# A gated cross-attention block on one core: one list of steps for all engines in place of a table of slots

## The reference

```python
def _L0_xattn_ref(query, context, ...):
    q = layer_norm(query, gq, betq)
    c = layer_norm(context, gkv, betkv)
    Q = (q @ Wq + bq) ; K = (c @ Wk + bk) ; V = (c @ Wv + bv)      # 16 heads
    attn = softmax(einsum('bhqd,bhkd->bhqk', Q, K) * SCALE)
    return einsum('bhqk,bhkd->bhqd', attn, V) @ Wo + bo
def _L0_ffn_ref(x, W1, b1, W2, b2):
    h = relu(x @ quantize(W1).T + b1)       # quantize: to -1, 0, 1 by a threshold on mean |W|
    return h @ quantize(W2).T + b2          # W1 2048 x 512, W2 512 x 2048
x = x + tanh(g_xattn[0]) * _L0_xattn_ref(_layernorm(x), ctx, ...)
x = x + tanh(g_ffn[0]) * _L0_ffn_ref(_layernorm(x), W1, b1, W2, b2)
```

## Time and profile before

| | |
|---|---|
| three runs | 1016.99, 1017.47, 1018.20 us; median 1017.47 us |
| the profiled execution | 1018.24 us, of which the span of instructions is 1016.4 us |
| PE busy | 917.1 us of the span, 90% |
| DVE, ACT, POOL busy | 735.9, 643.5, 307.8 us |
| mean granted clock of PE | 0.966 of full |

### The profile page before, as it was taken

How to read it: one execution, slowest core, us unless ns; L and a number is a source line. 1 busy time by engine, 2 the same in 40 slices (tenths; PEclk the granted TensorE clock), 3 DMA queues, 4 the chain that set the end, 5 groups by cost and what they waited for, 6 DMA issues and landing times.

```text
span 1016.4 us, 22463 instructions
## 1 busy us (share of the span) xinstructions
PE 917.1 (90%) x8994; PEld 704.0 (69%) x8994; DVE 735.9 (72%) x1358; ACT 643.5 (63%) x1330; POOL 307.8 (30%) x534
## 2 busy tenths in 40 slices
PE   3788898689999999999999999999999999889868
PEld 0444665466778778876788678876887677758747
DVE  4454699888777778777877877777877777788521
ACT  2765556755786567765795578756786576578411
POOL 4030265443250325122341325032412323033023
PEclk9798699889999999999999999999999999999969
DMA  9495925552211701251222411180223022210100
GB/s 292 129 247 132 217 75 143 144 147 39 50 38 46 172 21 41 62 150 33 60 63 66 117 41 39 45 182 7 55 62 101 2 60 62 65 38 1 37 4 19
DMA packets 56960, 84.02 MB, mean 83 GB/s; under 512 B 6376, under 2 KB 33448, under 8 KB 56856
## 3 DMA queue, kind: packets, MB, share of 16 engines
q1 hardware_dynamic: 50200, 65.80, 26.8%
q10 hardware_dynamic: 6656, 16.78, 5.6%
HBM read 42.20 MB, written 3.67 MB: 45 GB/s over the span
## 4 chain that ended last, share of the span: by engine, by line
PE 62%; DVE 8%; ACT 5%; POOL 2%; issue 1%; DMA 1%; SPq 1%; ACTq 0%
PE ps_fill L431 42%; PE ps_score L443 6%; PE ps_pv L472 5%; PE ps_exp L456 5%; DVE row_max L779 2%; PE ps_fill L482 2%; DVE p_parts L786 2%; ACT h_full L690 2%; PE ps_fill L524 1%; ACT ps_exp L642 1%; ACT ctx_raw L700 1%; POOL h_parts L1079 1%; DVE h_parts L882 1%; DMA x_residual<-x 1%; DVE rows_to_turn L804 1%
## 5 line engine op out<-in xcount | busy, mean ns | idle before, releaser
L640 ACT ACTIVATE p_parts<-ps_exp 125x448 f16<-125x448 f32 x384 | 209.0, 544 | 112.9 <-PE ps_exp L456 110.9
L779 DVE TENSOR_REDUCE row_max<-ps_score 128x1 f32<-128x750 f32 x256 | 237.9, 929 | 12.4 <-PE ps_score L443 10.1
L786 DVE TENSOR_TENSOR p_parts<-ps_exp,p_parts 125x448 f16<-125x448 f32 x384 | 235.5, 615 | 2.5 <-ACT ps_exp L642 2.5
L642 ACT ACTIVATE ps_exp<-ps_exp 125x448 f32<-125x448 f32 x384 | 210.8, 549 | 0.0
L443 PE MATMUL ps_score<-k_stack,q_stack 96*128 96x375 f16 x512 | 128.2, 332 | 43.1 <-DVE row_max L779 27.3
L456 PE MATMUL ps_exp<-q_stack,k_stack 99*125 99x224 f16 x768 | 141.3, 267 | 2.7 <-DVE p_parts L786 2.3
L456 PEld LDWEIGHTS ps_exp<-q_stack,k_stack 99*125 99x125 f16 x768 | 98.1, 140 | 35.4 <-DVE p_parts L786 9.0
L472 PE MATMUL ps_pv<-v_now,p_parts 125*128 125x66 f16 x3072 | 115.8, 194 | 1.1 <-DVE p_parts L786 1.1
L431 PE MATMUL ps_fill<-w_ternary,h_parts 128*128 128x256 fp8e4 x1024 | 116.5, 272 | 0.0
L472 PEld LDWEIGHTS ps_pv<-v_now,p_parts 125*128 125x128 f16 x3072 | 111.8, 98 | 1.2 <-issue 1.1
L431 PEld LDWEIGHTS ps_fill<-w_ternary,h_parts 128*128 128x128 f16 x1024 | 99.6, 98 | 11.2
(11 more groups left out here) (129 smaller groups left out, 1501.5 us busy)
## 6 DMA issues: line engine op xcount, KB each, us to landing
k_stack<-k_stage_hi SPq DMA_DIRECT2D x64, 187.5 KB, 2.7
v_now<-v_stage SPq DMA_DIRECT2D x32, 346.5 KB
ctx_raw<-ctx_in SPq DMA_DIRECT2D x8, 1344.0 KB
h_parts<-w1t ACTq DMA_DIRECT2D x16, 512.0 KB, 3.9
h_parts<-w2t ACTq DMA_DIRECT2D x16, 512.0 KB, 5.1
k_stack<-k_stage_lo SPq DMA_DIRECT2D x32, 187.5 KB, 3.2
x_for_q<-x SPq DMA_DIRECT2D x16, 256.0 KB, 11.1
x_residual<-x SPq DMA_DIRECT2D x16, 256.0 KB, 3.2
```

The costliest lines, as they stand in the source:

```text
L640: nc.scalar.activation(ph[0:KR, unit, :], ps_exp[0:KR, u, 0:2 * NQ], ACT.Exp, scale=EXP_SCALE)
L642: nc.scalar.activation(ps_exp[0:KR, u, 0:2 * NQ], ps_exp[0:KR, u, 0:2 * NQ], ACT.Exp, scale=EXP_SCALE).then_inc(exp_done, 1)
L779: nc.vector.tensor_reduce(mx[:, h, t:t + 1], ps_score[:, :, 0:KH], AX.XY, ALU.max) \
L786: nc.vector.tensor_tensor(pl[0:KR, unit, :], ps_exp[0:KR, u, 0:2 * NQ], ph[0:KR, unit, :], ALU.subtract).then_inc(p_split, 1)
```

## The change

The table of slots is gone. One list, `STEPS`, holds every step of the program as `kind.index@batch`: an opening of 791 steps, a round of 327 steps that is repeated for five batches, an ending of 330. Each engine walks the whole list and does its own part of what it finds. What was one step with a half on PE and ACT and a half on DVE is now two (`k` and `k_hi`, `cx` and `cx_lo`, `op` and `op_add`, `f2` and `f2_add`), the maximum is a step (`max`) apart from its `score`, the difference (`part`) apart from its `expo`, the sum of a `pv` is `take`, POOL's splitting of maxima is `split`; and every DMA is a step of SP: `kq`, `vc`, `ctx`, `x`, `xb`, `store`, `load`, `reload`.

Besides the order:

- PE no longer waits at the start of a body; each fill waits for the fill two ahead of it, and for nothing else of this kind.
- The 32 loads of weight pieces are issued by SP, not ACT. For the second pass they go through two buffers in place of three.
- The gates and the columns of small vectors are loaded by ACT's queue, ahead of everything; the rows `bo` and `b2` come after the weights.
- The first `rstd` and the last `rstd2` are done by DVE but for the power, which stays on POOL.
- `bo_sum` and `threshold` use `ps_fill`, the thresholds of W1 and W2 are made one by one, and the bias of q and k is turned by a DMA of its own.

The number of matmuls, of exponentials, of maxima and of comparisons is the same. The core of the diff:

```diff
-SLOT_WORK = [
-    [("q", 0), ("q", 1), ("mr", 1), ("bias", 0), ("divide", 0), ("k", 0)],
...
+ROUND = """
+    pv.12@-1 score.4@0 f2.2@-2 max.1@0 f2_add.0@-2 kq.1@0 part.36@-1 part.37@-1 take.11@-1 max.2@0 expo.42@-1 cx.4@1
...
+STEPS = steps_of(OPENING, 0)
+for _b in range(FIRST_ROUND, LAST_ROUND + 1):
+    STEPS += steps_of(ROUND, _b)
+STEPS += steps_of(ENDING, 0)
+FILLS = [s for s in STEPS if s[0] in FILL_KINDS]
+FILL_AT = {s: k for k, s in enumerate(FILLS)}
...
+                elif kind in FILL_KINDS:
+                    at = FILL_AT[kind, i, n]
+                    if at >= 2:
+                        pe.wait_ge(*freed(*FILLS[at - 2]))
+                    fill(kind, i, n, at % 2)
...
             def sum_piece(k):
 
-                act.wait_ge(piece_loaded[k % PIECE_RING], 16 * (k // PIECE_RING + 1))
-                nc.scalar.activation(piece[:, k % PIECE_RING, :], piece[:, k % PIECE_RING, :], ACT.Abs,
+                act.wait_ge(piece_loaded[k % 3], 16 * (k // 3 + 1))
+                nc.scalar.activation(piece[:, k % 3, :], piece[:, k % 3, :], ACT.Abs,
                                      accum_out=abs_sum[:, k:k + 1]).then_inc(piece_summed, 1)
-                act.wait_ge(piece_summed, k + 1)
-                load_piece(act, k + PIECE_RING)
...
+                elif kind == "rstd" and n == 0:
+                    variance_prep(dve, nc.vector, n)
+                    rstd_refine(dve, nc.vector, r1, rstd1_step, n * 8 + 2, mv1[:, :, 0], norm1_ready)
...
+                elif kind == "reload":
+                    if i < 2:
+                        sp.wait_ge(piece_summed, PIECES - 2 * i)
+                    else:
+                        sp.wait_ge(piece_compared, i - 1)
+                    load_piece(i, i % 2, piece_back)
...
+                elif kind == "store":
+                    sp.wait_ge(out_ready, n * 4 + 4)
```

More of the change, by code:

```diff
@@ new lines, with steps_of @@
+"""
+FILL_KINDS = ("bo_sum", "threshold", "cx", "xx", "q", "k", "v", "mr", "ot", "op", "yt", "f1", "f2")
+SECOND_HALF = {"bo_add": "bo_sum", "thr": "threshold", "cx_lo": "cx", "xx_lo": "xx", "q_hi": "q", "k_hi": "k",
+               "v_lo": "v", "ot_lo": "ot", "op_add": "op", "yt_lo": "yt", "f1_hi": "f1", "f2_add": "f2"}
+def steps_of(text, b):
+    found = [s.replace("@", ".").split(".") for s in text.split()]
+    return [(kind, int(i), b + int(n)) for kind, i, n in found if 0 <= b + int(n) < B]
@@ L422, in _ @@
+            sp.wait_ge(out_stored, B * 32)
         @block.tensor
@@ L675, in fill @@
                 elif kind == "v":
-                    if i == 0 and not (b == -1):
-                        act.wait_ge(v_landed[3], n * 32)
+                    if i == 0 and n:
+                        for c in range(DC):
+                            act.wait_ge(v_landed[c], n * 32)
                     nc.scalar.activation(v_stage[0:KR, i, :, 0, 0:HD],
@@ L768, in _ @@
-            act.wait_ge(bo_sums, 1)
-            iterations(body)
+            for kind, i, n in STEPS:
+                if kind == "expo":
+                    expo(i, n)
+                elif kind == "norm":
+                    norm(i, n)
+                elif kind == "w_hi":
+                    weight_hi(i)
+                elif kind == "piece_sum":
+                    sum_piece(i)
+                elif kind == "norm2":
+                    norm2(i, n)
+                elif kind in FILL_KINDS:
+                    at = FILL_AT[kind, i, n]
+                    fill(kind, i, n, at % 2, at + 1)
@@ L1010, in _ @@
-            dve.wait_ge(consts, 5)
-            nc.vector.memset(thr[:, :], 0.0).then_inc(out_ready, 4)
-            body(-2, OPEN)
-            body(-1, FIRST)
-            dve.wait_ge(thr_step, 2)
-            iterations(body)
+            dve.wait_ge(consts, 8)
+            nc.vector.memset(thr[:, :], 0.0)
+            for kind, i, n in STEPS:
+                if kind == "max":
+                    score(i, n)
+                elif kind == "part":
+                    part(i, n)
+                elif kind == "take":
+                    take_o(i, n)
+                elif kind == "stat":
+                    stat(i, n)
+                elif kind == "rstd" and n == 0:
+                    variance_prep(dve, nc.vector, n)
+                    rstd_refine(dve, nc.vector, r1, rstd1_step, n * 8 + 2, mv1[:, :, 0], norm1_ready)
+                elif kind == "rstd2" and n == B - 1:
+                    variance_finish(dve, nc.vector, n)
+                    rstd_refine(dve, nc.vector, r2, rstd2_step, n * 7 + 1, mv2[:, :, 0], norm2_ready)
+                elif kind == "gain":
+                    gain()
+                elif kind == "w_lo":
+                    weight_lo(i)
+                elif kind == "bias_row":
+                    bias_row(i)
+                elif kind == "tot":
+                    tot(i)
+                elif kind == "bias_ready":
+                    bias_ready(i)
+                elif kind == "ternary":
+                    compare(i)
+                elif kind == "divide":
+                    divide(n)
+                elif kind in SECOND_HALF:
+                    at = FILL_AT[SECOND_HALF[kind], i, n]
+                    fill(SECOND_HALF[kind], i, n, at % 2, at + 1)
```

899 lines of the change are left out of this document (420 added, 479 removed), and 13 rows, old and new, of tables (LAST_WORK, SLOT_WORK).

## The result

The changed kernel takes 971.43 us (median of 4 runs, 969.38 to 977.98) against 1017.23 us (4 runs); the ratio is 0.9564, 95% interval 0.9516 to 0.9613. The forecast was 971. That the sum came out so closely is in part luck: the first two stretches gave 2.2 and 2.9 us more than forecast and the last attention 5.4 us less. The changed kernel's own runs lie 8.6 us apart. The profiled execution has a span of 968.7 us.

The account below looks back on a forecast made before the run. It took PE as full in the rounds, DVE as pacing the first attention, and no engine as full in the set-up; -13 - 10 - 13 - 3 - 7 - 0.5 = -46.5 from 1018.24 gave 971.7, so 971 us, range 947 to 1000.

Parts of the forecast that it names:

- a: Set-up and first batch, 0 to 111.3 us, no engine full: -13 us from PE's waits, bounds 0 and -19.6.
- I take half, 3 us: In the set-up, moving all but the power of the first `rstd` from POOL to DVE gains 3 of 5.8 us.
- b: First attention and comparison of weights, 111.3 to 223.1 us, DVE sets the pace: -10 us, bounds -2 and -12.
- c: Five repeated rounds, 223.1 to 777.4 us, PE busy 539.6 of 554.3: -13 us, bounds 0 and -14.7.
- d: The stretch behind the five rounds, 777.4 to 883.3 us, 4.0 us of PE idle: -3 us.
- the two waits named: In each round, a score waiting for the context's lo part (1.4 us), and `mr` for POOL's split (0.9 us).
- the row of 109 ns: 32 matmuls of f2, 256 columns, 109 ns each at 2.4 GHz: without waits PE runs without a gap.
- e: Last attention beside the next-to-last feed-forward part, 883.3 to 963.2 us: -7 us, bounds -3 and -11.
- f: Last batch's output and feed-forward chain, 963.2 to 1016.4 us: -0.5 us from `rstd2`, bounds +0.5 and -2.
- The first (rounds don't gain): Rival: c and d give only 0 to 4 us, total 983 to 987, up to 1000; chance 0.15.
- The third: Rival: SP's order brings `x_residual` too late, stalling DVE and PE, some 1060 us; chance 0.06.
- The second: Rival: the set-up's wait for first weights shortens too and b reaches its 12; 945 to 958 us; chance 0.13.

Follow-up runs that it names:

- a3: The changed kernel with the first `rstd` and the last `rstd2` done by POOL as a whole, as before; 970.79 us, ratio 0.9539.
- a2: The changed kernel with the 16 first-pass loads of weight pieces issued by ACT again, ACT waiting for each sum; 988.14 us, ratio 0.9694.
- a8: The changed kernel, loads still on SP, with only ACT waiting after each of the 16 sums of a piece; 973.34 us, ratio 0.9559.
- a7: The changed kernel with batch 6's f1 and f2 doing only the first chunk, about 22 us of PE left out; 970.34 us, ratio 0.9550.
- a4: The changed kernel with SP holding back the load of `x_residual` until each repeated round's tenth `expo` is done; 1003.05 us, ratio 0.9851.

## Why the prediction was right, and where it was not

- **a, -13 against -15.2.** The sum held; its parts did not. "So I price waits alone" left out the clock: 10.4 us of the gain are idle time, less than the 13, and 4.8 are busy time, since no part of a runs at half the clock any more. The step "I take half, 3 us" for the first `rstd` failed: a3 shows 0, within a noise of about 2 us, and the 6.4 us that I read had DVE's work beside them, without which POOL takes 4.0. What I named and did not price, that ACT issues no loads, is enough to lose all of the gain when it is undone (a2: +18.4 us), and not by ACT's waits (a8; the 0.3 us of each issue were not tested alone), but by where the transfers go and what waits behind them. The 16.6 us for the first weights stayed, 17.1.
- **b, -10 against -12.9.** I took idle time alone as what can come back. It fell from 12.3 to 98.90 - 91.62 = 7.3 us, 5 us and not 10. The other 7.9 us are DVE's busy time. Some 3.3 of them are the two casts that met POOL in the kernel before (one of q, 2.21 us at 125.80, and the one of k in the earlier trace rows) and meet none now. That is the rule of the Trainium skill, "GPSIMD Engine Reference", section 1, which I weighed as speaking against the change; the page has it for DVE instructions in a two-port mode or with two SBUF inputs. The new order avoids the meetings. The rest is work that moved across the cut: two instructions of the comparisons, a cast of q, a maximum, a lo part and a statistic fewer stand in b, and a difference that only the late cut of the earlier trace rows had put there. That the first round gained 0.6 us where the others gained about 3 has another reason in part: the clock was at half for 3.4 us of it, and the same order without that took 108.4 to 109.7 us.
- **c and d, -13 and -3 against -13.2 and -3.9.** Right in kind, and the two waits named are shown to be 8.5 us of c. In size c was a little short: five other profiles of the same rounds give -15 to -16, at or past the bound of -14.7 that I took from PE's idle time, because its busy time in a round fell as well, from 107.9 to 107.4 us. The rule of the Trainium skill, "Perfetto Trace Analysis", section "Identifying the Most-Contended Engine", that the busy share of weight loads measures PE's room would have given rounds well below 107 us. PEld is 341.66 of 429.90 us now, 79%, and PE shows no wait: the trace speaks for the row of 109 ns.
- **e, -7 against -1.6** (-0.9 by equal cuts). This step failed: "79.9 - 68.8 = 11.1 us of PE idle; 5.9 of them in nine waits" took PE's idle time as a gain to be had. The waits moved: PE's for maxima went from 5.9 to 4.0 us, and DVE's for exponentials from 2.0 to 9.4. What stands there is a ring of PE, ACT and DVE with little else to fill it, and a7 shows that PE's work isn't its limit.
- **f, -0.5 against -0.9.** Below what can be told; a3 has 50.8 us with POOL alone.
- **The rivals.** The first (rounds don't gain) is out by c. The third is real as a mechanism (a4) and was avoided by 5 us. The second came half true: b gained more than its bound of -12, for another reason, and the first weights were as late as ever.
